# The y16 addition moves from VectorE to TensorE and ScalarE, and the tiles Bs and dl begin one element later

## The chip, the core and the metric

The kernel runs on one core of a Trainium2 chip: TensorE (PE), VectorE (DVE), ScalarE (ACT), GpSimd (POOL) and the DMA queue that SyncE (SP) issues. The metric is the device time of one execution in microseconds. Before the change it is 2680.79 us, the median of 3 runs (2679.48 to 2681.43).

## The reference, cut to what matters

The input x is 8 x 96 x 64 x 64. Layer 0 is a Mamba block over the 4096 positions of each image, layer 1 is a linear attention and a quantized feed-forward:

```python
# layer 0, per batch; 192 inner channels, 16 states
xz = groupnorm(x) @ in_proj_w.T;  xm, z = split(xz)
xm = silu(conv4(xm));  dt, B, C = split(xm @ x_proj_w.T)
delta = softplus(dt @ dt_proj_w.T + dt_proj_b)
h_t = exp(delta_t * A) * h_(t-1) + (delta_t * B_t) * xm_t     # for each channel and state
y_t = sum over states of h_t * C_t  + xm_t * D
x = x + layernorm((y * silu(z)) @ out_proj_w.T)
# layer 1, on tokens t
t = t + attn(ln(t))            # no softmax: (Q K^T) V, so a 96x96 matrix per batch does
h = relu(q16(q8(ln(t)) @ q8(W1).T + b1))                      # e5m2 products, f16 sums
t = t + q16(q16(q8(h) @ q8(W2).T) + q8(b2))
```

The last line is where the change is: the feed-forward's output, held in f16 as y16, is added to the rest of the sum.

## The kernel before

A batch's 4096 positions are cut into 8 chunks of T = 512, which makes 64 chunks in all. Each engine has one program, written out by hand as `iteration(g)` for g = -2 to 68, and runs it in that order; semaphores join the engines. In iteration g different chunks are at different stages: chunk g is scanned, g+1 and g+2 are projected, g-1 and g-2 go through layer 0's end, and g-10 to g-12 through layer 1 (its matrix is known only when a batch is complete, hence the lag).

The scan of a chunk has 24 blocks of 128 rows x 512 positions, in 6 groups (quads) of 4, named s and q. For each block ScalarE writes the decay exp(ds * A) into one of two PSUM banks (`decay`, L824, tile DA), VectorE scans it with the block's input (`scan`, L1194, R<-DA,R,D), and a decay waits until the scan two blocks earlier has freed its bank. The inputs of a quad, D = us * Bs, come from GpSimd for three quads (`inputs`, L640) and from VectorE for the other three (L1178, with Bs copied into the PSUM bank PB by ScalarE, L810). After a quad is scanned GpSimd multiplies it by Cs in place (`product`, L651), and TensorE sums the states into Y (`sum_states`, L1507 and L1511). GpSimd also makes du = dl * u once per chunk (L633); dl is the softplus of the step sizes, written by ScalarE (L796, L800) and clipped by VectorE (L1204). dl and du go out to DRAM and come back spread over the rows as ds and us; Bs and Cs come back from DRAM too.

The starts of the rows: R has rows of T+1 elements and is read by `product` from element 1 and written from element 0. D has rows of T+1 elements. Bs, Cs, us, ds, dl, du and u have rows of T or of 768 elements and begin at the start of their tiles.

Between the decays ScalarE does the rest of its work in a fixed order. In the stretch that the prediction speaks of it does decay (0,3), then `silu` (a table load, u, z, a table load: L773, L779, L780), then decays (1,0) and (1,1), `state_rows` (st, L787), `token_copy` (tT, L867), and decays (1,2) and (1,3). VectorE does scan (0,1), `token_norm` (th, L1233), scan (0,2), `inputs` (L1178), scan (0,3), `result` (xt, L1285), `gate` (yv, L1215), and then scans (1,0) to (1,3).

TensorE builds the sum of a finished chunk m = g-12 in the bank G2 with `x2_sum`: the attention's part (`x2_tokens`, L1625), and x1 by an f32 identity (`x2_x1`, L1628). VectorE's `result` then adds y16 and writes the output into the x1 tile, from which SyncE stores it. The bank G2 is free for `to_tokens` (L1563, tokens) when f_out tells that result is done. Behind x2_sum on TensorE's queue come the last quad's sum of states of chunk g-1 (L1511), x_proj of chunk g+1 (L1482 and L1484), and to_tokens.

Of the kernel before, what the change touches and what calls it, by code (L numbers as in the profile page):

```python
# [6 lines left out]
B, C, L = 8, 96, 4096  # L7
INNER, STATE, TAPS, RANK = 192, 16, 4, 6
HEADS, HIDDEN = 6, 384
T = 512  # L10
# [3 lines left out]
LOW = 128  # L14
# [17 lines left out]
W2 = T + H  # L32
# [24 lines left out]
def build(nc, I, cols, out):  # L57
# [7 lines left out]
    with ctx:  # L65
        def sb(name, shape, dt=f32):
            return ctx.enter_context(nc.sbuf_tensor(name, shape, dt))
# [31 lines left out]
        def there(k):  # L99
            return not known(k) or 0 <= k <= LAST  # L100
# [5 lines left out]
        def inside(k):  # L106

            return 0 <= k <= LAST - CH - OVER
# [74 lines left out]
        b1q = sb("b1q", [128, 3])  # L183
        b2q = sb("b2q", [C, 1])
        zero = sb("zero", [128, 4])
        epsn = sb("epsn", [128, 1])

        bst = sb("bst", [128, ROW // T, 6])
# [12 lines left out]
        u = sb("u", [LOW, 2, W2])  # L201
        z = sb("z", [LOW, ZS, W2])
        st = sb("st", [128, T])
        Bs = sb("Bs", [128, 2, 2, T])
        Cs = sb("Cs", [128, 2, 2, T])
        dl = sb("dl", [LOW, W2])
        du = sb("du", [LOW, W2])
        ds = sb("ds", [128, QUADS, T])
        us = sb("us", [128, QUADS, T])
# [28 lines left out]
        y16 = sb("y16", [C, T], f16)  # L238
# [113 lines left out]
        def x1_of(m):  # L352

            if known(m) and m == LAST:
                return x1[:, :]
            return xt[:, m % XS, :] if early(m) else tx[:, place(m), :]
# [326 lines left out]
        def _(act):  # L683
# [134 lines left out]
            def decay(k, s, q):  # L818
                j = QUAD * s + q
                if q == 0:  # L820
                    act.wait_ge(d_in[0 if s in LOWS else 1], count(k, 16, 16))
                act.wait_ge(scanned.sem, scanned.at(k, j + 1 - NDA))
                i = q if s in LOWS else QUAD + q % 2
                nc.scalar.activation(DA[j % NDA][:, :], ds[:, i, :], ACT.Exp,  # L824
                                     scale=A[:, j:j + 1]).then_inc(exp_done.sem, 1)
# [68 lines left out]
            def hidden_round(m):  # L894
# [2 lines left out]
                own_wait(nc.scalar)  # L897
                nc.scalar.activation(h8[:, :, :], h16[:, :, :], ACT.Relu, saturate=False).then_inc(f_h8.sem, 1)

            def output(m, src):  # L900
                act.wait_ge(f_down.sem, f_down.at(m))
                act.wait_ge(f_out.sem, f_out.at(m - 1))
                nc.scalar.copy(y16[:, :], src[0:C, :]).then_inc(f_y16.sem, 1)
# [5 lines left out]
            def iteration(g):  # L909
# [11 lines left out]
                    silu(g + 1)  # L921
                if there(g):
                    decay(g, 1, 0)
                    decay(g, 1, 1)
                if there(g + 1):
                    state_rows(g + 1, G0)
# [184 lines left out]
        def _(dve):  # L1111
            steps = [0]

            def step(ins):
                steps[0] += 1
                ins.then_inc(w_dve, 1)
                dve.wait_ge(w_dve, steps[0])
# [34 lines left out]
            step(nc.vector.tensor_scalar(w2q[:, :, :], w2f, 1.0, None, ALU.mult, saturate=False))  # L1152
            step(nc.vector.tensor_scalar(b1h[:, :], b1f, 1.0, None, ALU.mult, saturate=False))
            step(nc.vector.tensor_scalar(b2h[:, :], b2f, 1.0, None, ALU.mult, saturate=False))
            step(nc.vector.tensor_copy(b1q[:, :], b1h[:, :]))
            step(nc.vector.tensor_copy(b2q[:, :], b2h[:, :]))
            stats(1, gx_in[2:3])
# [124 lines left out]
            def result(m, o):  # L1282
                dve.wait_ge(f_x2.sem, f_x2.at(m))
                dve.wait_ge(f_yb.sem, f_yb.at(m))
                nc.vector.tensor_tensor(x1_of(m), o[0:C, :], y16[:, :], ALU.add).then_inc(f_out.sem, 1)  # L1285

            def iteration(g):
                if place(g + 3) == 0 and later(g + 3):
                    aggregate(g + 3)
                if there(g - 1):  # L1290
                    gate(g - 1, 0)
                if there(g):
                    scan(g, 0, 0)
                    scan(g, 0, 1)
                if there(g - 2):
                    token_norm(g - 2, G0)
                if there(g):
                    scan(g, 0, 2)
                    inputs(g, 1)
                if place(g - 10) == 0 and early(g - 10):  # L1300
                    fold(g - 10, 4, G1)
                if there(g):
                    scan(g, 0, 3)
                if inside(g - 12):
                    result(g - 12, G2)
                if there(g - 1):
                    gate(g - 1, 1)
                if there(g):
                    scan(g, 1, 0)
                    scan(g, 1, 1)  # L1310
                    scan(g, 1, 2)
                    scan(g, 1, 3)
                    scan(g, 2, 0)
                if there(g - 2):
                    gram(g - 2, G2)
                if there(g):
                    scan(g, 2, 1)
                if there(g + 1):
                    delta(g + 1, G3, G0)
                if there(g):  # L1320
                    scan(g, 2, 2)
                    inputs(g, 3)
                    scan(g, 2, 3)
                if there(g - 1):
                    scale_out(g - 1, G1)
                if there(g):
                    scan(g, 3, 0)
                if there(g - 1):
                    add_x(g - 1, G1)
                if there(g):  # L1330
                    scan(g, 3, 1)
                if place(g - 9) == 0 and early(g - 9):
                    fold(g - 9, 1, G0)
                if there(g):
                    scan(g, 3, 2)
                if inside(g - 10):
                    norm_x2(g - 10, G2)
                if place(g - 9) == 0 and early(g - 9):
                    fold(g - 9, 2, G3)
                if there(g):  # L1340
                    scan(g, 3, 3)
                    scan(g, 4, 0)
                    scan(g, 4, 1)
                    scan(g, 4, 2)
                    scan(g, 4, 3)
                    scan(g, 5, 0)
                    scan(g, 5, 1)
                if there(g + 1):
                    inputs(g + 1, 0)
                if there(g):  # L1350
                    scan(g, 5, 2)
                if place(g - 9) == 0 and early(g - 9):
                    fold(g - 9, 3, G2)
                if there(g):
                    scan(g, 5, 3)
# [69 lines left out]
        def _(pe):  # L1425
# [193 lines left out]
            def x2_sum(m, o):  # L1619
                x2_tokens(m, o)  # L1620
                x2_x1(m, o)

            def x2_tokens(m, o):
                landed(m)
                mm(o[0:C, :], MT[:, batch(m) % 2, 0, :], tokens_of(m), start=True, stop=False)  # L1625
# [20 lines left out]
            def iteration(g):  # L1646
# [8 lines left out]
                if inside(g - 12):  # L1655
                    ((place(g - 10) == 0 and freed(fold_ev, g - 10, 3)) or freed(f_h16, g - 11, 3)
                     or freed(post_ln, g - 2, 2) or freed(f_h16, g - 11, 1) or freed(f_q8, g - 11)
                     or freed(post_dve, g - 3, 4) or freed(post_act, g - 3, 5) or freed(f_out, g - 13))
                    x2_sum(g - 12, G2)
                if there(g - 1):  # L1660
                    sum_states(g - 1, 5)
                if there(g + 1):
# [298 lines left out]
```

## Time and profile before

| | |
|---|---|
| device time, median of 3 runs | 2680.79 us (2679.48 to 2681.43) |
| profiled execution, span from first to last instruction | 2683.3 us (the page gives no other time for it) |
| instructions | 34179 |
| DMA engines' mean busy share | 55% |
| mean granted TensorE clock | 0.910 |

How to read it: the profile is one execution on the chip. Rows of the timeline give the start, the time for which the instruction or the merged run of instructions (xN) lasted, the engine, the line of the kernel, the operation, and output <- inputs with shapes; in brackets is the idle time before it and what ended that. Neighbours on one engine overlap a little, so the distance from start to start is what an instruction costs its engine.

### The profile page before, as it was taken

To read this page: it belongs to the slowest core of one execution; us is meant where nothing else is said; L and a number is where in the kernel's file an instruction comes from. 1 tells how busy PE (TensorE), PEld (TensorE's weight loads), DVE (VectorE), ACT (ScalarE), POOL (GpSimd) and SP (SyncE) were. 2 spreads that over 40 slices of the span, in tenths; PEclk is the share of its full clock that TensorE was granted. 3 is DMA by queue.
4 is the path that set the end of the run, shared out by engine and by line. 5 is a ranking of instruction groups with operands and counts; after the bars stand their busy time and mean duration, and the time that the engine had idled before them with its cause. 6 is when DMAs were issued, how large, how long until landed. Compare 5 with 4: busy or idle time off the path is not lost.

```text
span 2683.3 us, 34179 instructions
## 1 busy us (share of the span) xinstructions
PE 2196.6 (82%) x9844; PEld 788.6 (29%) x9844; DVE 2603.7 (97%) x2503; ACT 2392.7 (89%) x3971; POOL 2576.9 (96%) x654
## 2 busy tenths in 40 slices
PE   6677777888888888888888888888888888888878
PEld 3222223323323323323323323323323322322323
DVE  7999999999999999999999999999999999999996
ACT  5677777999999999999999999999999999999976
POOL 4999999999999999999999999999999999999991
PEclk8788888889889899899989999899989989989978
DMA  6455555555555555555555556556556555555533
GB/s 247 157 176 167 172 173 175 185 184 193 197 185 188 202 184 193 197 185 196 194 185 205 184 188 199 187 190 205 183 191 199 185 192 192 177 194 194 169 124 79
DMA packets 171161, 494.44 MB, mean 184 GB/s; under 512 B 23040, under 2 KB 44672, under 8 KB 154144
## 3 DMA queue, kind: packets, MB, share of 16 engines
q1 hardware_dynamic: 170976, 492.25, 55.1%
q8 instruction: 82, 1.34, 0.2%
q14 instruction: 103, 0.84, 0.1%
HBM read 400.28 MB, written 91.88 MB: 183 GB/s over the span
## 4 chain that ended last, share of the span: by engine, by line
POOL 54%; issue 28%; DVE 11%; PE 3%; ACT 2%; DMA 1%; SPq 0%; POOLq 0%; DVEq 0%; ACTq 0%
POOL R L651 35%; POOL D L640 15%; DVE R L1194 7%; POOL du L633 4%; DVE D L1178 2%; ACT DA L824 1%; PE G L1430 1%; DMA R<-ths 1%; PE Y L1507 0%; PE G L1464 0%; DVE yv L1215 0%; ACT dl L796 0%; PE PB L1430 0%; DMA ds<-lo_d 0%; DVE G L1219 0%
## 5 line engine op out<-in xcount | busy, mean ns | idle before, releaser
L1194 DVE TENSOR_TENSOR_SCAN R<-DA,R,D 128x512 f32<-128x512 f32 x1344 | 1642.0, 1263 | 18.3 <-ACT DA L824 18.2
L651 POOL TENSOR_TENSOR R<-R,Cs 128x2048 f32<-128x2048 f32 x383 | 1593.3, 4187 | 0.0
L824 ACT ACTIVATE DA<-ds,kept_w 128x512 f32<-128x512 f32 x1536 | 1049.6, 687 | 198.7 <-DVE R L1194 183.5
L640 POOL TENSOR_TENSOR D<-us,Bs 128x2048 f32<-128x2048 f32 x193 | 877.6, 4547 | 15.4 <-DVE R L1194 7.8
L1178 DVE TENSOR_TENSOR D<-us,PB 128x2048 f32<-128x2048 f32 x191 | 431.4, 2259 | 5.8 <-ACT PB L810 5.6
L1507 PE MATMUL Y<-R,kept_w 128*32 128x512 f32 x2048 | 301.0, 674 | 43.8 <-POOL R L651 43.8
L1464 PE MATMUL G<-un,wcv 96*128 96x512 f32 x512 | 262.4, 660 | 20.5 <-ACT rs L835 10.7
L1511 PE MATMUL Y<-R,kept_w 128*32 128x256 f32 x2048 | 147.1, 407 | 100.2 <-POOL R L651 99.6
L1194 DVE TENSOR_TENSOR_SCAN R<-DA,D 128x512 f32<-128x512 f32 x192 | 222.4, 1203 | 4.6 <-ACT DA L824 4.6
L1430 PE MATMUL G<-sq,kept_w 96*96 96x512 f32 (+1 forms) x256 | 156.7, 697 | 78.9 <-ACT h L887 48.6
L1467 PE MATMUL G<-un,wcv 96*64 96x256 f32 x1024 | 173.0, 469 | 0.0
L1430 PE MATMUL G<-q,w1q 96*128 96x512 fp8e5 x164 | 71.4, 436 | 107.3 <-ACT rs L835 47.4
L1464 PEld LDWEIGHTS G<-un,wcv 96*128 96x128 f32 x512 | 101.2, 208 | 181.4 <-issue 112.0
L1430 PE MATMUL G<-st,kept_w 128*64 128x256 f32 (+1 forms) x384 | 112.5, 485 | 44.3 <-ACT st L787 44.3
L1507 PEld LDWEIGHTS Y<-R,kept_w 128*32 128x32 f32 x2048 | 47.0, 118 | 249.3 <-issue 145.4
L1511 PEld LDWEIGHTS Y<-R,kept_w 128*32 128x32 f32 x2048 | 55.6, 113 | 206.2 <-POOL R L651 178.8
L633 POOL TENSOR_TENSOR du<-dl,u 128x768 f32<-128x768 f32 x63 | 115.3, 1831 | 0.0
L1467 PEld LDWEIGHTS G<-un,wcv 96*64 96x64 f32 x1024 | 72.1, 157 | 145.6 <-issue 129.3
L1430 PE MATMUL G<-un,kept_w 96*128 96x512 f32 x372 | 110.3, 485 | 4.1 <-DVE gk L1268 2.7
L891 ACT ACTIVATE h<-h,b1q 128x512 f16<-128x512 f16 x165 | 111.9, 711 | 0.0
L810 ACT COPY PB<-Bs 128x512 f32<-128x512 f32 x191 | 110.1, 577 | 0.0
L1518 PE MATMUL Y<-u,kept_w 128*128 128x512 f32 x128 | 103.0, 900 | 0.0
(223 smaller groups left out, 3217.7 us busy)
## 6 DMA issues: line engine op xcount, KB each, us to landing
Bs<-bc_d SPq DMA_DIRECT2D x128, 512.0 KB, 4.3
us<-lo_d SPq DMA_DIRECT2D x64, 1024.0 KB, 6.8
ds<-lo_d SPq DMA_DIRECT2D x64, 1024.0 KB, 7.2
Cs<-bc_d SPq DMA_DIRECT2D x128, 512.0 KB, 4.9
us<-hi_d SPq DMA_DIRECT2D x64, 512.0 KB, 6.4
ds<-hi_d SPq DMA_DIRECT2D x64, 512.0 KB, 5.1
lo_d<-dl SPq DMA_DIRECT2D x64, 256.0 KB, 2.0
lo_d<-du SPq DMA_DIRECT2D x64, 256.0 KB, 2.0
```

Of the source, the lines that this page charges most:

```text
L633: nc.gpsimd.tensor_tensor(du[:, :], dl[:, :], u[:, place(k) % 2, :], ALU.mult)\
L640: nc.gpsimd.tensor_tensor(shaped(D[:, s % NDBU, :, :], s), low(us, s) if s in LOWS else high(us), of_states(Bs, s), ALU.mult).then_inc(don ...
L651: nc.gpsimd.tensor_tensor(shaped(R[:, s, :, 0:T], s), shaped(R[:, s, :, 1:S], s), of_states(Cs, s), ALU.mult).then_inc(hc_done.sem, 1)
L824: nc.scalar.activation(DA[j % NDA][:, :], ds[:, i, :], ACT.Exp, scale=A[:, j:j + 1]).then_inc(exp_done.sem, 1)
L891: nc.scalar.activation(h16[:, n, :], h16[:, n, :], ACT.Identity, bias=b1q[:, n:n + 1])\
L1178: nc.vector.tensor_tensor(D[:, s % NDBU, :, :], low(us, s), PB[:, :].unsqueeze(1).to_broadcast([128, QUAD, T]), ALU.mult)\
L1194: nc.vector.tensor_tensor_scan(R[:, s, q, 1:S], DA[j % NDA][:, :], D[:, s % NDBU, q, :], before, ALU.mult, ALU.add).then_inc(scanned.sem, 1)
L1430: return mm(o, left, right, start=True, stop=True)
L1464: last = mm(o[:, :], wcv[:, t, 0:LOW], un[:, t:t + T], start=(t == 0), stop=(t == TAPS - 1))
L1467: last = mm(o[rows, 0:H], wcv[:, t, LOW:LOW + HIGH], un[:, t + cs.start:t + cs.stop], start=(t == 0), stop=(t == TAPS - 1))
L1507: last = mm(Y[32 * q:32 * q + 32, :], sumsel, R[:, s, q, 0:T], start=s == 0, stop=s == 3)
L1511: last = mm(Y[at:at + 32, 0:H], sumsel, R[:, s, q, cs], start=False, stop=s == 5 and q > 1)
```

## The change

y16 is now added on TensorE: `whole_sum` waits for the biased y16 and multiplies it by an f16 identity (id16, cast once from the f32 identity) into the same PSUM sum. A new `result` on ScalarE copies the bank into the x1 tile, between decays (1,0) and (1,1), and VectorE's `result` is no longer called in `iteration` (the ending of the program still uses it). It holds for the 52 chunks that `iteration` finishes. Bs and dl begin one element into tiles that are 16 elements longer.

```diff
+        id16 = sb("id16", [C, C], f16)
...
-        Bs = sb("Bs", [128, 2, 2, T])
+        Bs = sb("Bs", [128, 4 * T + 16])[:, 1:1 + 4 * T].rearrange("p (h w t) -> p h w t", h=2, w=2)
         Cs = sb("Cs", [128, 2, 2, T])
-        dl = sb("dl", [LOW, W2])
+        dl = sb("dl", [LOW, W2 + 16])[:, 1:1 + W2]
...
+            def result(m, src):                                  # ScalarE
+                act.wait_ge(f_x2.sem, f_x2.at(m))
+                nc.scalar.copy(x1_of(m), src[0:C, :]).then_inc(f_out.sem, 1)
...
                 if there(g):
                     decay(g, 1, 0)
+                if inside(g - 12):
+                    result(g - 12, G2)
+                if there(g):
                     decay(g, 1, 1)
...
+            step(nc.vector.tensor_copy(id16[:, :], ident))
...
                 if there(g):
                     scan(g, 0, 3)
-                if inside(g - 12):
-                    result(g - 12, G2)
                 if there(g - 1):
                     gate(g - 1, 1)
...
+            def whole_sum(m, o):                                 # TensorE
+                x2_tokens(m, o)
+                mm(o[0:C, :], ident, x1_of(m), start=False, stop=False)
+                pe.wait_ge(f_yb.sem, f_yb.at(m))
+                mm(o[0:C, :], id16[:, :], y16[:, :], start=False, stop=True).then_inc(f_x2.sem, 1)
...
-                    x2_sum(g - 12, G2)
+                    whole_sum(g - 12, G2)
```

ScalarE's queue from decay (0,3) of a chunk to decay (1,2) before the change (DA0 and DA1 are the two decay banks):

```order
L824 ACTIVATE DA1<-ds,kept_w 128x512
L773 ACT_TABLE_LOAD
L773 ACTIVATE u<-raw 128x768
L779 ACTIVATE z<-raw 128x768
L780 ACT_TABLE_LOAD
L824 ACTIVATE DA0<-ds,kept_w 128x512
L824 ACTIVATE DA1<-ds,kept_w 128x512
L787 ACTIVATE st<-G0,kept_w 128x512
L867 COPY tT<-G2 128x4x96
L824 ACTIVATE DA0<-ds,kept_w 128x512
```

The same place in the changed kernel, whose lines up to here are numbered one higher:

```order
L825 ACTIVATE DA1<-ds,kept_w 128x512
L774 ACT_TABLE_LOAD
L774 ACTIVATE u<-raw 128x768
L780 ACTIVATE z<-raw 128x768
L781 ACT_TABLE_LOAD
L825 ACTIVATE DA0<-ds,kept_w 128x512
L903 COPY xt<-G2 96x512
L825 ACTIVATE DA1<-ds,kept_w 128x512
L788 ACTIVATE st<-G0,kept_w 128x512
L868 COPY tT<-G2 128x4x96
L825 ACTIVATE DA0<-ds,kept_w 128x512
```

The copy stands between the two decays that follow the Silu stretch, so decay (1,1), st, tT and decay (1,2) are queued behind it. On TensorE, in the same iteration, the changed kernel's queue from the new matmul on:

```order
L1634 MATMUL G2<-y16,id16 96x512
L1518 MATMUL Y<-R,kept_w 32x256 x8
L1489 MATMUL G0<-u,kept_w 128x512
L1491 MATMUL G0<-u,kept_w 128x256 x2
L1570 MATMUL G2<-kept_w,th 128x96 x4
```

The new matmul stands ahead of the last sum of states, x_proj and the tokens, whose order among themselves is the old one.

## Rows read from the trace of the kernel before

**Rows 1.** The page: busy time of each engine, its share, instructions.

```profile
PE 2196.6 (82%) x9844; PEld 788.6 (29%) x9844; DVE 2603.7 (97%) x2503; ACT 2392.7 (89%) x3971; POOL 2576.9 (96%) x654
```

**Rows 2.** Windows: stretch, length, busy us per engine (instructions), clock, DMA, GB/s.

```profile
1345.00:1666.00 321.00, 269.45 (x1232) 95.70 (x1231) 319.40 (x302) 305.52 (x515) 320.76 (x81) 0.94 0.57 192
```

**Rows 3.** The chain of waits from 1400 to 1440 us, by line.

```profile
by line: POOL R L651 54.7%; issue 31.4%; POOL D L640 20.3%; POOL du L633 4.6%; POOLq L639 0.2%; POOLq L632 0.1%; POOLq L645 0.0%
```

**Rows 4.** VectorE's waits, 1345 to 1666 us: total, times, longest.

```profile
DVE gp L1270 <- PE G L1430: 0.7, 1, 0.7
DVE yv L1215 <- PE Y L1507: 0.6, 1, 0.6
```

**Rows 5.** Instructions by form, GpSimd: busy us, mean ns, idle before.

```profile
L651 POOL TENSOR_TENSOR R<-R,Cs 128x2048 f32<-128x2048 f32 x383 | 1593.3, 4187 | 0.0
L640 POOL TENSOR_TENSOR D<-us,Bs 128x2048 f32<-128x2048 f32 x193 | 877.6, 4547 | 15.4 <-DVE R L1194 7.8 <-DMA us<-lo_d 7.6
L633 POOL TENSOR_TENSOR du<-dl,u 128x768 f32<-128x768 f32 x63 | 115.3, 1831 | 0.0
...
L620 POOL TENSOR_TENSOR du<-dl,u 128x512 f32<-128x512 f32 x1 | 1.3, 1267 | 27.0 <-DVE dl L1204 27.0
```

**Rows 6.** Lines 751 and 830: ns minimum/median/maximum, first and last start, forms.

```profile
L751 ACT ACTIVATE un<-un,cgs x63: 803/814/822, 24.2 to 2506.4; 96x515 f32<-96x515 f32 x56, 96x512 f32<-96x512 f32 x7
...
L830 ACT ACTIVATE sq<-G x126: 575/585/595, 91.1 to 2595.1; 96x512 f32<-96x512 f32 x126
```

**Rows 7.** DMA issues: KB each, median us to landing.

```profile
un<-in_x SPq DMA_DIRECT2D x56, 193.1 KB, 4.3
...
un<-in_x SPq DMA_DIRECT2D x8, 192.0 KB, 4.2
```

**Rows 8.** Timeline of VectorE, 1448 to 1455 us.

```profile
1448.78 0.66 DVE L1233 TENSOR_TENSOR th<-G,rs 96x512 f32<-96x512 f32 x1
...
1453.93 0.66 DVE L1285 TENSOR_TENSOR xt<-G,y 96x512 f32<-96x512 f32 x1
1454.51 0.41 DVE L1215 TENSOR_TENSOR yv<-Y,z 128x256 f32<-128x256 f32 x1
1454.84 5.97 DVE L1194 TENSOR_TENSOR_SCAN R<-DA,R,D 128x512 f32<-128x512 f32 x5
```

**Rows 9.** Timeline of ScalarE, 1448 to 1456 us.

```profile
1448.90 0.69 ACT L824 ACTIVATE DA<-ds,kept_w 128x512 f32<-128x512 f32 x1 [0.41 <-DVE R L1194]
...
1450.90 0.84 ACT L773 ACTIVATE u<-raw 128x768 f32<-128x768 f32 x1
...
1453.79 1.30 ACT L824 ACTIVATE DA<-ds,kept_w 128x512 f32<-128x512 f32 x2
1455.03 0.67 ACT L787 ACTIVATE st<-G,kept_w 128x512 f32<-128x512 f32 x1
1455.60 0.46 ACT L867 COPY tT<-G 128x384 f32<-128x384 f32 x1
```

**Rows 10.** Timelines of VectorE, ScalarE and TensorE in an early chunk, 326 to 329 us.

```profile
328.81 6.19 DVE L1194 TENSOR_TENSOR_SCAN R<-DA,R,D 128x512 f32<-128x512 f32 x5 [0.19 <-ACT DA L824]
...
328.08 1.30 ACT L824 ACTIVATE DA<-ds,kept_w 128x512 f32<-128x512 f32 x2
...
326.67 2.07 PE L1482 MATMUL G<-u,kept_w 128*128 128x512 f32 x2
```

**Rows 11.** Timeline of TensorE, 1449 to 1455 us.

```profile
1449.14 1.02 PE L1628 MATMUL G<-xt,kept_w 96*96 96x512 f32 x2
1451.34 1.07 PE L1511 MATMUL Y<-R,kept_w 128*32 128x256 f32 x16 [1.17 <-POOL R L651]
1452.34 1.12 PE L1482 MATMUL G<-u,kept_w 128*128 128x512 f32 x2
...
1454.65 0.55 PE L1563 MATMUL G<-kept_w,th 96*128 96x96 f32 x4 [0.32 <-DVE xt L1285]
```

**Rows 12.** Windows, the first 12 chunks.

```profile
55.00:541.00 486.00, 372.58 (x1662) 135.18 (x1660) 465.76 (x424) 368.02 (x590) 480.21 (x120) 0.84 0.52 172
```

## The prediction

> **What bounds the kernel now.** I read the busy shares first, then one steady batch, then the chain, the waits and the timelines. VectorE is busy 97% of the span, GpSimd 96%, ScalarE 89% [rows 1]: two engines without air, and which of them sets the pace is open. A stretch of 321 us, in which one batch of 8 chunks runs, has GpSimd busy for 320.76 us and VectorE for 319.40 [rows 2]. The chain of waits between 1400 and 1440 us stays on GpSimd's queue: its products, inputs and du, with "issue" between them [rows 3]. VectorE's idle 1.6 us of the batch are mostly one wait of 0.7 for the fold and one of 0.6 for Y [rows 4]. So GpSimd is the bound by a hair, and VectorE stands 1.4 us per batch behind it. Work taken off VectorE alone buys nothing; work taken off GpSimd alone buys at most 1.4 us per batch, 0.2 per chunk. The change touches both.
>
> **GpSimd: the two moved starts.** Per chunk GpSimd runs 6 products R<-R,Cs, 3 inputs D<-us,Bs and one du<-dl,u, all f32 multiplications; products and inputs have 2048 elements each. Yet a product takes 4187 ns and an input 4547 [rows 5]. What differs is where the two reads begin. `product` reads R from element 1 of rows of 513, so for q = 0 to 3 it begins 1, 2, 3 and 0 elements past a multiple of four, and Cs begins on one: three rows of four are out of step. In `inputs` us and Bs both begin on a multiple of four, and in du so do dl and u. The write side doesn't explain it: D has rows of 513, du has not, and their rates agree. du with 512 elements takes 1267 ns, the input with 2048 takes 4547 [rows 5]: (4547 - 1267) / 1536 = 2.14 ns per element and 0.17 us that depends on no size; du with 768 should then take 1814 and takes 1831. The product gives (4187 - 170) / 2048 = 1.96.
>
> Bs one element on puts all four rows of an input out of step. No row shows just that, so I bound it. If the out-of-step rows alone are fast and q = 3 costs 2.14, a fast row costs (4 x 1.96 - 2.14) / 3 = 1.90, and the input 0.17 + 2048 x 1.90 = 4.06 us. If it is R as the first operand that matters and not the step between the two, the input stays at 4.55. No f32 multiplication in the trace is slower per element than the present input, so no gain at all is the dear end. I take the product's 4.19, the nearest row: 0.36 us less for each of 3 inputs, 1.08 per chunk. For du it is 768 x (2.14 - 1.96) = 0.14. GpSimd's demand falls by 1.22 us per chunk, 9.8 per batch, from 320.8 to 311. It stops being the bound, and would do so at 0.2 us per chunk; the exact rate hardly matters.
>
> Here a rule speaks against the change. The products, with two f32 inputs, ran at 1.96 ns per element [rows 5]. The Trainium skill, "GPSIMD Engine Reference", section 3 (Performance versus the Vector engine), gives 4497 ns for a 2048-element add and calls about 2.5 cycles per element the floor of any two-input operation, since both reads share one port. By that rule the start of a tile gives nothing and the sum ends at no change. The page's figure fits the inputs' 4547; the products' 4187 lie under its floor, and that measurement is why I side with the step between the operands.
>
> The other readers and writers of Bs and dl are ScalarE's copy of Bs, its Exp and Ln into dl, VectorE's min and max on dl, and the DMAs. ScalarE's pass over un has two forms, 512 elements from element 3 and 515 from element 0, and all 63 take 803 to 822 ns [rows 6]: an odd start costs it nothing visible. The DMA into un from element 3 (192.0 KB) lands in 4.2 us, that from element 0 in 4.3 [rows 7]. I cost all of this at 0; and a Bs load a few tenths longer would be hidden: GpSimd, which reads Bs, is idle for only 0.24 us of the whole batch [rows 2].
>
> **VectorE loses the addition, ScalarE gets a copy.** xt<-G,y goes from VectorE in 52 chunks, 0.58 us each (1453.93 to 1454.51 [rows 8]). If VectorE could use all of it, its demand would fall by 8 x 0.58 = 4.6 per batch. It can't. Take the chunk at 1446 us [rows 8, 9]. ScalarE's fourth decay (1448.90) waited for VectorE's second scan; then come two table loads and two Silus, and the fifth decay starts at 1453.79, 4.89 later. This way hangs on VectorE's own scan and moves with it. VectorE in the meantime does th, scan, D<-us,PB, scan, xt, yv, from 1448.78 to 1454.84. Without xt it is ready at 1454.26, the decay only at 1453.79 + 0.69 + 0.04 = 1454.52 (0.04 by the scan at 328.81, which waited for the decay of 328.08 [rows 10]). So 0.32 of the 0.58 is got here. That early chunk, which has no y16 addition yet, shows just this wait, 0.19 us.
>
> Now the copy, behind the fifth decay. Its f_x2 comes from matmuls that end about 1450.2 [rows 11], 1450.5 with the f16 one: no wait. Its price: sq<-G, also 96x512 out of PSUM, takes 585 ns [rows 6]; by the rows of 9 a ScalarE instruction starts about 0.1 before the end of the one ahead (st at 1455.03, 0.67 long, tT at 1455.60), so it holds the engine for some 0.48. Queued behind it are decay 6, st, tT and decay 7, and VectorE's scans wait for the decays. Decay 6 starts at 1454.41 + 0.48 = 1454.89 and is ready at 1455.62; its scan wants it at 1454.52 + 1.19 = 1455.71, just in time. st follows at 1455.51, tT at 1456.08, decay 7 at 1456.44, ready at 1457.17. Its scan started at 1454.84 + 2 x 1.19 = 1457.22 before and would want it at 1456.90 now. Another quarter is gone: of 0.58, 0.05 us per chunk is left. Behind decay 7 ScalarE is where it was.
>
> In the first chunk of a batch scans take 0.06 less each, VectorE's way is 0.2 shorter and ScalarE's the same: there the stretch gets about 0.15 longer. In the chunk with the fold, VectorE's copy to MT in this stretch, some 0.27 us, fits into the wait. VectorE's batch is 319.4 - 7 x 0.05 - 0.27 + 0.15 = 318.9, plus its waits: the 0.6 for Y goes (TensorE got it from GpSimd's product), the 0.7 for the fold stays. 319.6 against 321: 1.4 us per batch, 0.18 per chunk, over 52 chunks 9.
>
> **TensorE.** One f16 matmul 96x512 more per chunk, with a wait for y16, which was written a chunk earlier. Two f32 ones of that width take 1.02 us together [rows 11], so it costs between 0.2 and 0.5. Behind it stands the last sum of states, which now waits 1.17 us for GpSimd [rows 11]. With a faster GpSimd this cover shrinks, but x_proj behind it needs u (1450.90 + 0.84 [rows 9]), later than all of this. tokens (L1563) waits for the result, which comes from ScalarE at 1454.99 instead of from VectorE at 1454.59; it ends at about 1455.6, before ScalarE asks for it at 1456.08, 0.47 to spare. Cost 0.
>
> **First 12 chunks and the end.** From 55 to 541 us GpSimd is busy for 480.21 of 486 and VectorE for 465.76 [rows 12]; there is hardly a y16 addition in it. GpSimd falls by 12 x 1.22 to 466, level with VectorE, whose 20 us of idle time would then be the limit. What part of it goes with GpSimd's lead no row tells: between 0 and 20 us, I take 5, because the convolutions that come late at the granted clock of 0.84 stay late. At the end GpSimd's last products come about 1 us earlier. The cast to id16 is done once, beside the loading of weights: 0.
>
> **Sum.** 9 + 5 + 1 = 15 us off the profiled span, 2683.3 to 2668. The page gives no other time of that execution; its span is 2.5 us above the median of the timed runs, 2680.8, which gives 2665.8, rounded to 2665.
>
> **Rivals.**
> 1. GpSimd's inputs stay at 4.55 us, because only R's odd start as first operand is fast. Then GpSimd stays the bound at 320.8 per batch, and what VectorE gains is slack. For it: no row has an odd start in second place. Against: du would have its odd start in first place, and the products' rate. Time 2681, 2678 to 2683. The floor of the Trainium skill's page would end here too.
> 2. The full gain: ScalarE isn't the limit in the Silu stretch. Batch 314.8 + 0.7 = 315.5, 5.3 us less, 0.67 per chunk, 35 over 52 chunks, with 5 to 10 for the beginning: 2638. For it: ScalarE is idle for 15 us of each batch [rows 2]. Against: its fourth decay waits for a scan, and from there its way has no air.
> 3. Slower: the token chain. tT stands before decay 7 on ScalarE, waits for L1563 on TensorE, and that now waits for ScalarE's copy. It decides as soon as L1563 ends over 0.47 us later than worked out. At half clock, as in the early chunk where x_proj's first two took 2.07 instead of 1.12 [rows 10, 11], x_proj (u ready at 1451.74) ends at 1455.9 and L1563 at 1456.9; tT, decay 7 and its scan come 0.8 late: a chunk of 40.7 us against 40.1. In every chunk that is +30 us, in half of them about +15: 2695. For it: part of each batch runs at half clock, 0.94 on average [rows 2]. Against: in the chunk at 1446 us x_proj ran at full rate.
>
> **How the numbers follow.** Forecast 0.54 (its own range 2655 to 2675), rival 1 0.19, rival 2 0.14, rival 3 0.13. Differences within 0.2% (2675.4 to 2686.2) are what a measurement of this kernel can't tell from none. Faster by more: 0.97 of the forecast and rival 2, 0.66; within: rival 1 and the rest of the forecast, 0.21; slower 0.13. The range, 2638 to 2690, leaves out half of rival 2 and the larger part of rival 3.
>
> **What would show it.** Right: inputs near 4.19 us and du near 1.69; GpSimd idle for VectorE's scans some 8 us per batch; VectorE waiting for DA twice in each chunk, about 0.26 us each, at the fifth and the seventh decay's scan. Wrong: inputs at 4.55 (rival 1); VectorE without those waits (rival 2); tT waiting for L1563 (rival 3); or GpSimd waiting for a Bs load, which would make the DMA's odd start the step that failed.

## The result, and the profile after

The changed kernel took 2690.02 us (median of 5 runs, 2686.87 to 2693.43) against 2680.79 for the kernel before, run beside it (5 runs, 2679.48 to 2682.14). The ratio is 1.0036 with a 95% interval of 1.0025 to 1.0047: slower, by a little more than the 0.2% that the prediction set as the bound of no change. The forecast said 2665, and its range, 2638 to 2690, ends just below the measured time. The profiled execution has a span of 2688.1 us, 4.8 above that of before, at a mean granted clock of 0.907 (before 0.910).

The page of the changed kernel gives for busy time, in the columns of [rows 1]:

```profile
PE 2201.5 (82%) x9896; PEld 805.0 (30%) x9896; DVE 2585.0 (96%) x2452; ACT 2407.0 (90%) x4023; POOL 2442.9 (91%) x654
```

GpSimd has fallen from 96% to 91%, more than forecast; VectorE has only fallen from 97% to 96%, with its 52 additions gone. Its busy time is 19 us less and the kernel still takes longer: the new time is pauses. (In all timelines xN counts the trace's records. Line 1489 is one f32 matmul of the program per chunk and stands there as x2, down's three fp8 matmuls as x3.) The chain of waits from 1400 to 1440 us, by line, answers to [rows 3]; it starts:

```profile
by line: DVE R L1203 35.5%; issue 16.3%; DVE D L1187 10.9%; PE G L1437 6.6%; PE Y L1514 4.7%; PE G L1579 3.5%; ACT DA L825 3.2%; ACT L781 3.2%; PE G L1656 3.0%; ACT L774 2.7%; PE G L1535 2.2%; PE G L1533 2.1%; ACT u L774 2.1%; ACT z L780 1.
```

It was on GpSimd alone before; now it is on VectorE's scans and, where these pause, goes through ScalarE to TensorE. GpSimd's operations by form, with the columns of [rows 5]:

```profile
L652 POOL TENSOR_TENSOR R<-R,Cs 128x2048 f32<-128x2048 f32 x383 | 1592.3, 4172 | 45.6 <-DVE R L1203 45.0
L641 POOL TENSOR_TENSOR D<-us,Bs 128x2048 f32<-128x2048 f32 x193 | 735.2, 3809 | 94.3 <-DVE R L1203 85.9 <-DMA us<-lo_d 8.0 <-issue 0.4
L634 POOL TENSOR_TENSOR du<-dl,u 128x768 f32<-128x768 f32 x63 | 114.1, 1811 | 12.3 <-DVE dl L1213 12.0
```

The inputs went from 4547 to 3809 ns (forecast 4190, bounds 4060 to 4550: better than the good bound), du from 1831 to 1811 (forecast 1690: no gain). GpSimd is now ahead and idle for VectorE's scans, 131 us in the two rows.

Of the waits (us in total, times, longest), three are new or larger; line 1203 is the scan (1194 before), 825 the decay, 903 the new copy, 908 the cast of the down matmuls' sum to y, 1570 the tokens and 1656 the down matmuls:

```profile
PE G L1570 <- ACT xt L903: 59.8, 52, 1.2
...
DVE R L1203 <- ACT DA L825: 53.5, 149, 2.0
...
ACT y L908 <- PE G L1656: 47.5, 53, 2.5
```

Before, scans waited for a decay 22.7 us in all (38 times) and the cast for the down matmuls 7.9 us (10 times). The steady part, 50 chunks between the same two points of the program, is 541 to 2547 us before and 534 to 2551 after; the last line is the first 12 chunks after:

```profile
541.00:2547.00 2006.00, 1685.23 (x7686) 598.17 (x7686) 1995.88 (x1881) 1898.56 (x3165) 2004.01 (x501) 0.94 0.57 191
...
534.00:2551.00 2017.00, 1699.16 (x7733) 617.57 (x7734) 1977.51 (x1829) 1911.01 (x3214) 1900.32 (x501) 0.93 0.58 190
55.00:534.00 479.00, 364.68 (x1661) 132.87 (x1661) 464.68 (x422) 368.02 (x590) 454.33 (x120) 0.85 0.52 174
```

The first 12 chunks take 479 us against 486 [rows 12], a gain of 7 where 5 were forecast. The steady part takes 2017 us against 2006: 11 more where 9 fewer were forecast. To see where, I added up VectorE's pauses of more than 0.05 us between one instruction and the next, sorted by what stands behind them. Each pause counts against the usual distance of the two: neighbours normally overlap, after a scan by some 0.08 us, so a pause is that much longer than its bracket. In the 50 steady chunks before they are 11.7 us. After they are 50.4: 12.7 us ahead of the fifth decay's scan (in 44 chunks), 15.2 ahead of the seventh's (in all 50), 0.29 and 0.30 each where 0.26 and 0.27 were forecast, and 20.4 us in 25 chunks ahead of the ninth decay's scan, where nothing was forecast. VectorE saves 50 x 0.58 = 29 us and pauses 38.7 more: 10 of the 11 us.

One chunk with the third wait, on VectorE, ScalarE and TensorE from 1530 to 1540 us (start, length, engine, line, operation, count, in brackets the wait and its releaser):

```profile
1532.10 2.46 DVE L1203 TENSOR_TENSOR_SCAN R<-DA,R,D 128x512 f32<-128x512 f32 x2 [0.20 <-ACT DA L825]
1534.82 2.46 DVE L1203 TENSOR_TENSOR_SCAN R<-DA,R,D 128x512 f32<-128x512 f32 x2 [0.26 <-ACT DA L825]
1538.49 1.28 DVE L1203 TENSOR_TENSOR_SCAN R<-DA,R,D 128x512 f32<-128x512 f32 x1 [1.21 <-ACT DA L825]
```

```profile
1532.01 0.57 ACT L903 COPY xt<-G 96x512 f32<-96x512 f32 x1
...
1534.95 0.69 ACT L825 ACTIVATE DA<-ds,kept_w 128x512 f32<-128x512 f32 x1
1537.28 0.58 ACT L908 CAST y<-G 96x512 f16<-96x512 f32 x1 [1.65 <-PE G L1656]
1537.76 0.69 ACT L825 ACTIVATE DA<-ds,kept_w 128x512 f32<-128x512 f32 x1
```

```profile
1529.48 1.10 PE L1489 MATMUL G<-u,kept_w 128*128 128x512 f32 x2 [0.58 <-ACT u L774]
...
1530.41 1.03 PE L1491 MATMUL G<-u,kept_w 128*128 128x256 f32 x4
1532.64 0.55 PE L1570 MATMUL G<-kept_w,th 96*128 96x96 f32 x4 [1.20 <-ACT xt L903]
...
1533.92 2.04 PE L1437 MATMUL G<-st,kept_w 128*128 128x512 f32 x2 [0.42 <-ACT st L788]
1535.76 1.49 PE L1656 MATMUL G<-h,w2q 128*96 128x512 fp8e5 x3
```

Read TensorE's rows from the top. TensorE finishes x_proj (lines 1489 and 1491) and stands idle for 1.20 us until ScalarE's copy is there. Behind the tokens it runs some small matmuls on group statistics, which only one chunk in eight has. Its next large matmul, dt_proj's first, takes 2.04 us, and the three down matmuls 1.49. ScalarE's cast waits 1.65 us for them, the ninth decay stands behind the cast, and VectorE's scan waits 1.21 us for that decay. In the kernel before the same place reads:

```profile
1454.65 0.55 PE L1563 MATMUL G<-kept_w,th 96*128 96x96 f32 x4 [0.32 <-DVE xt L1285]
1455.84 1.10 PE L1430 MATMUL G<-st,kept_w 128*128 128x512 f32 x2 [0.65 <-ACT st L787]
1456.78 0.81 PE L1643 MATMUL G<-h,w2q 128*96 128x512 fp8e5 x3
```

There 1.10 and 0.81 us are the same matmuls at the higher of the two levels, 2.4 GHz; 2.04 and 1.49 are near twice that, the level of 1.2 GHz. The granted clock of the bad chunk's 10 us was 0.83, that of an undisturbed chunk of the same run 1.00:

```profile
1530.00:1540.00 10.00, 8.38 (x37) 4.48 (x36) 8.34 (x10) 8.32 (x18) 8.21 (x3) 0.83 0.55 165
1486.00:1496.00 10.00, 7.62 (x40) 3.21 (x39) 9.61 (x10) 9.13 (x13) 9.44 (x3) 1.00 0.84 242
```

Over the steady part the down matmuls run slow (1.24 to 1.49 us) in 25 of 50 chunks, the same 25 in which the ninth decay's scan waits, and dt_proj's first matmul takes over 1.4 us in 14 of them; before, in none. The tokens wait 1.20 us in 48 of the 50. In the other two they wait 0.24, and nothing is slow there.

### The profile page after: what moved, and what is told of

It reads as the page before. It is cut to its first block, busy times and chain, and to the rows that moved or that the text cites. A ratio compares the mean times of both kernels' runs of the same rounds, so it can differ in the third digit from the quotient of the medians.

```text
span 2688.1 us, 34232 instructions
## 1 busy us (share of the span) xinstructions
PE 2201.5 (82%) x9896; PEld 805.0 (30%) x9896; DVE 2585.0 (96%) x2452; ACT 2407.0 (90%) x4023; POOL 2442.9 (91%) x654
## 4 chain that ended last, share of the span: by engine, by line
DVE 43%; ACT 19%; issue 17%; PE 10%; POOL 9%; DMA 1%; SPq 0%; ACTq 0%; DVEq 0%; POOLq 0%
DVE R L1203 30%; DVE D L1187 8%; POOL R L652 5%; ACT DA L825 5%; PE G L1437 4%; POOL D L641 3%; ACT L781 2%; ACT L774 2%; PE G L1656 2%; ACT u L774 2%; ACT dl L797 1%; ACT z L780 1%; DVE xq L1234 1%; ACT st L788 1%; DVE yv L1224 1%
## 5 line engine op out<-in xcount | busy, mean ns | idle before, releaser
L1203 DVE TENSOR_TENSOR_SCAN R<-DA,R,D 128x512 f32<-128x512 f32 x1344 | 1649.8, 1266 | 44.7 <-ACT DA L825 44.3
L641 POOL TENSOR_TENSOR D<-us,Bs 128x2048 f32<-128x2048 f32 x193 | 735.2, 3809 | 94.3 <-DVE R L1203 85.9
L1514 PE MATMUL Y<-R,kept_w 128*32 128x512 f32 x2048 | 285.1, 648 | 16.4 <-POOL R L652 16.4
L1471 PE MATMUL G<-un,wcv 96*128 96x512 f32 x512 | 263.0, 661 | 20.4 <-ACT rs L836 10.6
L1437 PE MATMUL G<-st,kept_w 128*64 128x256 f32 (+1 forms) x384 | 133.2, 570 | 55.0 <-ACT st L788 55.0
L1474 PE MATMUL G<-un,wcv 96*64 96x256 f32 x1024 | 163.4, 447 | 0.0
L634 POOL TENSOR_TENSOR du<-dl,u 128x768 f32<-128x768 f32 x63 | 114.1, 1811 | 12.3 <-DVE dl L1213 12.0
L1514 PEld LDWEIGHTS Y<-R,kept_w 128*32 128x32 f32 x2048 | 48.3, 116 | 205.4 <-issue 142.3
L1528 PE MATMUL Y<-u,kept_w 64*64 64x256 f32 x256 | 44.7, 428 | 75.0 <-DVE yv L1224 74.8
L1489 PE MATMUL G<-u,kept_w 128*128 128x512 f32 x128 | 77.2, 687 | 27.0 <-ACT u L774 26.9
```

The costliest lines, as they stand in the source:

```text
L634: nc.gpsimd.tensor_tensor(du[:, :], dl[:, :], u[:, place(k) % 2, :], ALU.mult)\
L641: nc.gpsimd.tensor_tensor(shaped(D[:, s % NDBU, :, :], s), low(us, s) if s in LOWS else high(us), of_states(Bs, s), ALU.mult).then_inc(don ...
L1203: nc.vector.tensor_tensor_scan(R[:, s, q, 1:S], DA[j % NDA][:, :], D[:, s % NDBU, q, :], before, ALU.mult, ALU.add).then_inc(scanned.sem, 1)
L1437: return mm(o, left, right, start=True, stop=True)
L1471: last = mm(o[:, :], wcv[:, t, 0:LOW], un[:, t:t + T], start=(t == 0), stop=(t == TAPS - 1))
L1474: last = mm(o[rows, 0:H], wcv[:, t, LOW:LOW + HIGH], un[:, t + cs.start:t + cs.stop], start=(t == 0), stop=(t == TAPS - 1))
```

## The experiments

The theory from this profile: (A) the moved starts gain, the moved addition brings two foreseen waits that eat its gain, and on top TensorE's idle time before the tokens drops it to half clock, by which down, cast and ninth decay come late. Rivals: (B) the moved starts themselves cost something; (C) ScalarE's order behind the copy is simply full, so that a wait taken away in one place comes back in the next. The expectations call the blocks (s, q): decay (1,0) is the fifth, (1,2) the seventh and (2,0) the ninth. All were run beside the kernel before; "pauses" are the sum explained above.

### The starts alone

```
 (kernel before)
+ Bs = sb("Bs", [128, 4*T + 16])[:, 1:1 + 4*T].rearrange(...)
+ dl = sb("dl", [LOW, W2 + 16])[:, 1:1 + W2]
```

> Only the starts of Bs and dl are moved; the y16 addition stays on VectorE. Theory A (GpSimd's faster inputs free the kernel from GpSimd's pace, and all the loss of the change comes from the move to TensorE and ScalarE): inputs at 3.8 us as in the changed kernel, VectorE becomes the bound at its old demand of 39.9 us per chunk, the waits for Y go, the first 12 chunks gain the 6 us that the changed kernel gained there: 2665 to 2673. Theory B (the moved starts themselves cost something, by the Bs loads that landed in 5.5 us instead of 4.3, or by GpSimd hitting VectorE more): at or above 2681, with VectorE's waits or longer scans to show for it.

Measured: 2664.04 us (5 runs), ratio 0.9940 (0.9927 to 0.9954). That is 1 us below A's range. Pauses 2.0 us, no slow down matmul. Its page:

```profile
PE 2174.4 (82%) x9844; PEld 783.4 (29%) x9844; DVE 2602.0 (98%) x2503; ACT 2392.4 (90%) x3971; POOL 2441.4 (92%) x654
```

VectorE is at 98% and has hardly a pause left: it is the bound. B has fallen; the starts are worth 16 us. The chain that ended last still names GpSimd for 69% of this run. At 92% busy GpSimd is not the limit; the chain only shows who came last by a hair.

### The addition alone

```
 (changed kernel)
- Bs = sb("Bs", [128, 4*T + 16])[:, 1:1 + 4*T].rearrange(...)
+ Bs = sb("Bs", [128, 2, 2, T])
- dl = sb("dl", [LOW, W2 + 16])[:, 1:1 + W2]
+ dl = sb("dl", [LOW, W2])
```

> Only the y16 addition is moved; Bs and dl begin where they did. Theory A: GpSimd is the bound again at 40.05 us per chunk, so the 0.58 us that VectorE saves is slack and gains nothing; the copy and TensorE's f16 matmul push st, dt_proj, down and the y cast back, now with x_proj later as well because it comes behind GpSimd's last product: 2685 to 2700, and VectorE waits for decay (2,0) in many chunks. Theory B (the loss comes from the starts): no slower than before, 2676 to 2683.

Measured: 2680.59 us (11 runs), ratio 1.0003 (0.9995 to 1.0012): no change, and A's number missed. Pauses are 40.0 us, but GpSimd is the bound and they cost nothing. And no down matmul ran slow. TensorE in a chunk of it:

```profile
1492.17 1.07 PE L1518 MATMUL Y<-R,kept_w 128*32 128x256 f32 x16 [0.96 <-POOL R L652]
1493.17 1.13 PE L1489 MATMUL G<-u,kept_w 128*128 128x512 f32 x2
1494.13 1.03 PE L1491 MATMUL G<-u,kept_w 128*128 128x256 f32 x4
1495.77 0.55 PE L1570 MATMUL G<-kept_w,th 96*128 96x96 f32 x4 [0.61 <-ACT xt L903]
1497.05 1.10 PE L1437 MATMUL G<-st,kept_w 128*128 128x512 f32 x2 [0.73 <-ACT st L788]
1497.99 0.81 PE L1656 MATMUL G<-h,w2q 128*96 128x512 fp8e5 x3
```

Here TensorE's idle time lies in two halves, 0.96 ahead of the last sum of states (for GpSimd's product) and 0.61 ahead of the tokens. With a faster GpSimd the first goes. TensorE then waits for u instead (0.58 ahead of line 1489 in the chunk at 1530 us), which is there sooner, so x_proj ends sooner too, while the copy comes no earlier: 1.20 before the tokens. This kernel has the wait of 1.20 in three of its 50 steady chunks and a shorter one or none in the others. So the loss comes neither from the starts (-16 us alone) nor from the addition (0 alone) but from the two together: -16 and 0 make +9.

### The cast behind the ninth decay

```
 (changed kernel, ScalarE)
-                if inside(g - 11):
-                    output(g - 11, G1)
 ...                decay(g, 2, 0)
+                if inside(g - 11):
+                    output(g - 11, G1)
```

> The changed kernel with one swap on ScalarE: the y cast, which waits for down on TensorE, comes behind decay (2,0) instead of ahead of it. Theory A (the waits before scan (2,0), 20 us in 25 of 50 chunks, come from the y cast waiting for down in front of that decay): those waits go, 20 us less, 2668 to 2674, and the two waits of 0.28 us in each chunk stay. Theory C (ScalarE as a whole is late at that place, because st, tT and the decays behind the copy are): the wait before scan (2,0) only moves to scan (2,1), 2685 to 2690.

Measured: 2685.73 us (11 runs), ratio 1.0021 (1.0012 to 1.0029), at C's number. The cast's wait fell from 47.5 to 7.4 us, the down matmuls were still slow in 17 chunks, and the wait moved on: 10.7 us ahead of the tenth decay's scan in 39 chunks and 7.6 in 17 ahead of VectorE's first operation on gram's result (lines 1266 and 1268). So about as much came back behind the ninth decay as had gone ahead of it, as C says. On VectorE:

```profile
1533.42 3.63 DVE L1203 TENSOR_TENSOR_SCAN R<-DA,R,D 128x512 f32<-128x512 f32 x3 [0.26 <-ACT DA L825]
1536.97 0.23 DVE L1268 TENSOR_TENSOR G<-G 97x97 f32<-97x97 f32 x1
1537.37 1.28 DVE L1203 TENSOR_TENSOR_SCAN R<-DA,R,D 128x512 f32<-128x512 f32 x1 [0.17 <-ACT DA L825]
```

The ninth decay's scan is in time (third of the three). Giving the late matmuls more room doesn't cure it while they are slow. Why they are slow C doesn't say: that is the question of the next two runs.

### The down matmuls ahead of the tokens

```
 (changed kernel, TensorE)
+                if inside(g - 11):
+                    ...
+                    down(g - 11, G1)
                 if there(g - 2):
                     to_tokens(g - 2, G2)
 ...
-                if inside(g - 11):
-                    ...
-                    down(g - 11, G1)
```

> The changed kernel with one move on TensorE: the three down matmuls come ahead of the tokens, in the 1.2 us in which TensorE waits for ScalarE's copy, instead of behind st and the first dt_proj. Theory A: down is finished before the y cast asks for it in every chunk, ScalarE's wait for it (43 us in 49 of 50 chunks) and VectorE's wait before scan (2,0) go, 2668 to 2674. Theory C: as for the swap, the wait moves to the next scan, 2685 to 2690. If the granted clock matters more than the order (half clock from here on because TensorE sat idle), the idle time that is filled raises it above 0.907 and the time falls below 2668.

Measured: 2664.98 us (5 runs), ratio 0.9941 (0.9929 to 0.9954): 25 us below the changed kernel, by one group of three matmuls moved up. TensorE, then ScalarE:

```profile
1521.85 0.81 PE L1656 MATMUL G<-h,w2q 128*96 128x512 fp8e5 x3
1523.21 0.55 PE L1570 MATMUL G<-kept_w,th 96*128 96x96 f32 x4 [0.55 <-ACT xt L903]
...
1524.49 1.68 PE L1437 MATMUL G<-st,kept_w 128*128 128x512 f32 x6 [0.42 <-ACT st L788]
```

```profile
1526.13 0.59 ACT L908 CAST y<-G 96x512 f16<-96x512 f32 x1
```

The idle time before the tokens is 0.55 instead of 1.20, no down matmul is slow, and the cast doesn't wait in the steady part. Pauses are 29.4 us, of which 27.9 are the two waits that the prediction had. The time is below 2668 and the granted clock of the profiled execution is 0.918 against 0.907, which is the expectation's third case. With the missed mechanism gone the forecast comes out, and in its parts too: the 50 steady chunks take 11 us less than before (9 forecast) and the first 12 take 6 less (5 forecast). But this experiment does two things: it fills the idle time, and it takes the down matmuls from behind the slow stretch.

### The idle time filled, down where it was

```
 (changed kernel, TensorE, ahead of to_tokens)
+                    spin(2, G1, *weights)
```

Two f32 matmuls whose result nobody reads, over the bank that down overwrites.

> The changed kernel, down where it was, and two f32 matmuls of 256 columns without use put ahead of the tokens, in the 1.2 us in which TensorE waits for ScalarE's copy (into the bank that down overwrites afterwards). Theory A1 (TensorE falls to half clock at dt_proj and down, 25 downs of 50 at 1.5 us instead of 0.8, because it stood idle there just before; the order alone costs nothing): the downs run at full clock, the wait before scan (2,0) goes, 2665 to 2670. Theory A2 (the order is what costs, down stands behind st and dt_proj): the y cast and scan (2,0) wait as in the changed kernel, 2685 to 2690, or more by what the idle matmuls take.

Measured: 2669.21 us (5 runs), ratio 0.9954 (0.9941 to 0.9968), in A1's range. TensorE:

```profile
1524.00 1.03 PE L1437 MATMUL G<-kept_w 128*128 128x256 f32 x4
1525.36 0.55 PE L1570 MATMUL G<-kept_w,th 96*128 96x96 f32 x4 [0.34 <-ACT xt L903]
1525.75 0.48 PE L1437 MATMUL PB<-mv,kept_w 128*128 128x1 f32 x4
1526.65 1.10 PE L1437 MATMUL G<-st,kept_w 128*128 128x512 f32 x2 [0.42 <-ACT st L788]
1527.58 0.81 PE L1656 MATMUL G<-h,w2q 128*96 128x512 fp8e5 x3
```

TensorE does more and the kernel is 21 us faster. Every steady dt_proj and down matmul is at full clock, in the place where down was slow in half of the chunks. ScalarE's cast still waits for them (21.7 us over 48 waits), but the ninth decay's scan never does. This settles that the idle stretch ahead of them, and not their place, costs the 20 us.

### The copy behind the group of decays

```
 (down matmuls first; ScalarE)
-                    result(g - 12, G2)       # behind decay (1, 0)
 ...
-                    token_copy(g - 2, G2)
 ...
                     decay(g, 1, 2); decay(g, 1, 3)
+                    result(g - 12, G2)
 ...                 decay(g, 2, 0); output(g - 11, G1)
+                    token_copy(g - 2, G2)
 (TensorE: tokens behind dt_proj; VectorE: gram one scan later)
```

> From the version with down first: ScalarE's copy stands behind decay (1,3) instead of behind decay (1,0), tT behind the y cast, and on TensorE the tokens behind both dt_proj; VectorE's gram addition comes one scan and the clipping of dl later. If the two waits of 0.28 us in the Silu stretch are what eats the 0.58 us that VectorE saves, the one before scan (1,2) goes and 0.3 us per chunk are gained: 2648 to 2656. If instead ScalarE is late behind the stretch (decays (2,0) and (2,1)) or TensorE is held by the later gram, it stays at 2662 to 2675.

Measured: 2743.59 us (4 runs), ratio 1.0236 (1.0222 to 1.0250). Both numbers missed by far. VectorE:

```profile
1521.68 5.99 DVE L1203 TENSOR_TENSOR_SCAN R<-DA,R,D 128x512 f32<-128x512 f32 x5 [0.19 <-ACT DA L825]
1528.37 1.28 DVE L1203 TENSOR_TENSOR_SCAN R<-DA,R,D 128x512 f32<-128x512 f32 x1 [0.70 <-ACT DA L825]
...
1536.54 1.28 DVE L1203 TENSOR_TENSOR_SCAN R<-DA,R,D 128x512 f32<-128x512 f32 x1 [0.43 <-ACT DA L825]
```

The wait of the seventh decay's scan is gone: five scans run in one piece. But the tenth decay now stands behind cast, token copy and dl's Exp, and its scan waits 0.70 (35.8 us in the brackets of all 50 steady chunks); further on ScalarE's fsq waits 1.30 for the matmuls of centre_x2, which use the bank that the moved gram addition frees, and a decay stands behind it (its scan waits 0.43, 19.9 us over 49 chunks). Pauses: 93.6 us. So this shift of the copy takes one foreseen wait away and brings larger ones, as C says. Other places for it were not tried.

### GpSimd's starts by themselves

A kernel that does nothing of the computation but f32 multiplications on GpSimd, three of each kind, with chosen starts of first operand, second operand and output (one execution):

```
O[:, o:o+2048] <- A[:, a:a+2048] * V[:, v:v+512] repeated 4 times
```

> A kernel of its own that leaves the whole computation out: GpSimd alone, f32 multiplications of 2048 and 768 elements with first operand, second operand and output starting 0 to 8 elements into their tiles, each form three times. If the step between the two reads counts: 4.5 us with both at 0 or both at 1, 3.8 with one of them at 1 or 3, whichever it is, and 4.5 again at 4 and 8 (if multiples of four are what it goes by; at 2 it tells four from two). If the second operand alone counts: 3.8 only with that one at 1. For du (768 elements), which gained nothing in the changed kernel with its first operand at 1: 1.81 with the first at 1, and about 1.55 with the second at 1 if operands differ, or about 1.8 in both if the size or the output's start matters.

By form, for (a, v, o) = (0,0,0), (0,1,0), (0,2,0), (0,3,0), (2,0,0), (0,0,1) and the product's form (rows of 513, v = 0), in this order:

```profile
L91 POOL TENSOR_TENSOR O<-A,V 128x2048 f32<-128x2048 f32 x3 | 13.5, 4495 | 11.2 <-DMA O<-in_x 11.0
...
L93 POOL TENSOR_TENSOR O<-A,V 128x2048 f32<-128x2048 f32 x3 | 11.4, 3812 | 0.2
...
L95 POOL TENSOR_TENSOR O<-A,V 128x2048 f32<-128x2048 f32 x3 | 11.4, 3815 | 0.2
...
L97 POOL TENSOR_TENSOR O<-A,V 128x2048 f32<-128x2048 f32 x3 | 13.5, 4499 | 0.2
...
L105 POOL TENSOR_TENSOR O<-A,V 128x2048 f32<-128x2048 f32 x3 | 11.4, 3812 | 0.2
...
L109 POOL TENSOR_TENSOR O<-A,V 128x2048 f32<-128x2048 f32 x3 | 13.5, 4496 | 0.2
...
L129 POOL TENSOR_TENSOR A<-A,V 128x2048 f32<-128x2048 f32 x3 | 12.5, 4154 | 0.2
```

There are two speeds, 4.50 and 3.81 us. All 19 kinds without rows of 513 in the first operand fall in line with one rule: v - a, modulo four elements, is 1 or 2 where it takes 3.81 us and 0 or 3 where it takes 4.50; the output's start does nothing. The product has two rows of each, and (4.50 + 3.81) / 2 = 4.15. At 768 elements the two speeds are 1.80 and 1.55 us, and du with a = 1, v = 0 takes the 1.80. The expectation had 1 and 3 as the fast starts of either operand; it is 1 and 2, and which operand is moved counts.

### dl three elements on

```
 (the starts alone)
- dl = sb("dl", [LOW, W2 + 16])[:, 1:1 + W2]
+ dl = sb("dl", [LOW, W2 + 16])[:, 3:3 + W2]
```

> The kernel before with Bs one element on, as in the run of the starts alone (2664.0), and dl three elements on instead of one. GpSimd's du reads dl first and u (start 0) second. In the run of the starts alone the step from the first operand's start to the second's is 0 - 1 = 3 mod 4 and du took 1.81 us; here it is 0 - 3 = 1 mod 4. If the step decides (measured on GpSimd alone: 768 elements 1.80 us at steps 0 and 3, 1.545 at 1 and 2), du takes about 1.55 us. If an odd first start is what counts, du stays at 1.81. On the time: by the theory that VectorE alone sets the pace once Bs is moved, 0.26 us per chunk off GpSimd buy nothing: 2661 to 2667. If GpSimd still holds something up, up to 64 x 0.26 = 17 us: 2647 to 2658.

Measured: 2662.26 us (4 runs), ratio 0.9934 (0.9917 to 0.9951), which overlaps with that of the starts alone. GpSimd:

```profile
L633 POOL TENSOR_TENSOR du<-dl,u 128x768 f32<-128x768 f32 x63 | 97.4, 1546 | 0.0
```

1546 ns as the rule says, and no measurable time from 17 us of GpSimd's work: VectorE is the bound. This kernel, the starts alone and the down matmuls first all beat the kernel before and the changed one, and can't be told apart.

## Why the prediction was wrong

- **The failed step** is the TensorE paragraph, "Cost 0", together with "Behind decay 7 ScalarE is where it was". I followed TensorE up to the tokens, found 0.47 us to spare, and stopped. The tokens' part held: in the undisturbed chunk (TensorE, then ScalarE) the tokens end at 1493.15 and tT starts at 1493.64.

```profile
1492.60 0.55 PE L1570 MATMUL G<-kept_w,th 96*128 96x96 f32 x4 [1.20 <-ACT xt L903]
```

```profile
1493.64 0.46 ACT L868 COPY tT<-G 128x384 f32<-128x384 f32 x1
```

  What lies behind the tokens wasn't asked: a pause before them of 1.20 us instead of 0.32, and what TensorE's clock does behind it. It cost 20.4 us of VectorE's pauses directly, and 25 us of the kernel's time between the changed kernel and the one with down first.
- **Rival 3** had the right engine, the half clock and the sign, but another place: x_proj slow, tokens and tT late, decay 7 late. x_proj's first matmul was never slow in the steady part (1.10 to 1.13 us). After the change the stretch that follows the idle time is dt_proj and down, and the chain goes on through the cast and the ninth decay. I looked for slow matmuls where the trace of before had them, instead of where the change makes TensorE idle. At 13 in 100 it was given too little. That its 2695 is near the 2690 measured is luck: it added 15 us to the time of before, while the slow matmuls cost 25 on top of 2665.
- **The link between the two edits** was half seen. I wrote that with a faster GpSimd the wait of 1.17 us ahead of the last sum of states shrinks, and took it as harmless. It was: but the idle time doesn't vanish, it moves to the places ahead of x_proj (0.58 us) and ahead of the tokens (1.20). The new matmul itself took 0.38 us, within the 0.2 to 0.5 forecast, though the "two f32 ones" it was worked out from are the two records of one.
- **GpSimd's inputs and du**: sizes off (3.81 for 4.19; no gain for 0.14), because I took "out of step" as one class. Of the product's four rows two are fast and not three: 2 x 1.96 - 2.14 = 1.78 ns per element for a fast row, and 0.17 + 2048 x 1.78 = 3.82 us, against 3.81 measured. GpSimd's demand fell by 2.2 us per chunk and not by 1.22. The Trainium skill, "GPSIMD Engine Reference", section 3, measures 4497 ns for an addition of 2048 elements and calls about 2.6 cycles per element the floor of two-input operations; the multiplications of 4.50 us here agree with it, those of 3809 ns in this kernel lie below it. As forecast, the exact rate hardly mattered once GpSimd was no longer the bound.
- **VectorE and ScalarE in the Silu stretch**: right. Two waits per chunk, 0.20 to 0.26 in the brackets, 0.29 and 0.30 in the tally; of the 0.58 of the addition 0.02 is left, where 0.05 was forecast.
- **First 12 chunks and end**: 5 forecast, 7 measured; right in kind.
- **The Sum**: 2665 forecast. With the missed mechanism taken out 2664.98 was measured (that the two agree so closely is luck, since single runs of that kernel lie between 2662.5 and 2667.8), and the starts alone give 2664.04. So the moved addition buys nothing beside the starts: 29 us saved on VectorE, 28 lost in two waits.

What stays open: in 48 of 50 steady chunks the tokens wait 1.20 us, but down is slow in 25 only. With the cast behind the ninth decay it is 17 of 40, and the addition alone has three such pauses (at 774, 1415 and 2378 us), without a slow matmul. No down matmul of the steady part is slow without such a pause ahead of it, in any of the runs. What tells the slow chunks apart no row shows. The Trainium skill, "TensorE: Matmul & The Clock Gate", section "A second HAM failure mode: psum-queue depth-cycling", tells of a kernel whose short idles between groups of matmuls make the clock swing between its two levels. The runs here agree: down ran at the lower level in 25 chunks with the pause of 1.20 us, and in none with the pause filled.

## What to carry to other kernels

When an edit makes an engine wait longer, follow that engine past the wait: what it runs next may be slower, and whoever queues behind that result is where the time goes. Two edits that are harmless each can gather their idle times in one place; run each alone before the pair. Work taken from the busiest engine is worth only what the path through its neighbour leaves, here 0.02 of 0.58 us.

## What the hardware showed that I had not expected

- GpSimd's f32 multiplication of 2048 elements has two speeds, 4.50 and 3.81 us, set by the distance of the second operand's start from the first's modulo four elements (1 or 2 fast, 0 or 3 slow), whatever the output's start.
- TensorE ran the same f32 matmul in 1.10 or in 2.04 us behind an idle time of 1.20 us, and two useless matmuls in that gap made the kernel 21 us faster.
- The DMA loads of Bs, 512 KB each, land in a median of 4.8 to 5.5 us in the seven runs with the tile one element on (5.5 in the changed kernel, 5.4 in the starts alone) and in 4.3 in the two without. Why, no run shows. In the changed kernel no wait for these loads shows.
